# A full-attention stage rewritten per pair of 64-wide heads, with row-tiled scores and column-tiled weighted values

## The reference

```
def _L1_attn_ref(x, Wq, Wk, Wv, Wo, bo):
    S, D, H, DH, SCALE = 256, 128, 16, 64, 64 ** -0.5
    q = (x @ Wq).reshape(b, s, H, DH)      # Wq, Wk, Wv: 128 x 1024
    k = (x @ Wk).reshape(b, s, H, DH)
    v = (x @ Wv).reshape(b, s, H, DH)
    scores = jnp.einsum('bqhd,bkhd->bhqk', q, k) * SCALE
    attn = jax.nn.softmax(scores, axis=-1)
    out = jnp.einsum('bhqk,bkhd->bqhd', attn, v).reshape(b, s, H * DH)
    return out @ Wo + bo                   # Wo: 1024 x 128

x = x + _L1_attn_ref(_layernorm(x, axis=-1), ...)   # no scale or shift in the norm
```

## Time and profile before

| | before |
|---|---|
| median of 3 runs | 5669.12 us (5667.3 to 5673.87) |
| profiled execution, its own time | 5667.65 us |
| its span, first to last instruction | 5665.8 us |
| granted TensorE clock over the span | 0.962 |
| PE busy | 4785.3 us (84%) |
| DVE busy | 4254.1 us (75%) |
| ACT busy | 3789.1 us (67%) |

### The profile page before, as it was taken

One profiled execution on the slowest core, in us unless ns is written; L12 is line 12 of the kernel. 1 busy time (PEld: TensorE's weight loads), 2 busy tenths in 40 slices (PEclk: granted clock), 3 DMA queues, 4 the chain that ended last, 5 costly groups with the idle time before them and its releaser, 6 DMA issues.

```text
span 5665.8 us, 133229 instructions
## 1 busy us (share of the span) xinstructions
PE 4785.3 (84%) x47928; PEld 3219.6 (57%) x48122; DVE 4254.1 (75%) x6024; ACT 3789.1 (67%) x7196; POOL 2480.3 (44%) x1142
## 2 busy tenths in 40 slices
PE   3349999999958888888888888888888888888886
PEld 1124478888835555555555555555555555555554
DVE  6761155566678888888888888888888888888886
ACT  3323255555547777777777777777777777777775
POOL 0100000000046565665656656565665656566564
PEclk7669999999979999999999999999999999999998
DMA  2000000000010000000000000000000000000001
GB/s 59 0 0 0 0 20 0 0 0 0 0 39 0 0 0 0 19 0 0 0 0 19 0 0 0 4 15 0 0 0 19 0 0 0 0 19 0 0 0 34
DMA packets 43314, 34.86 MB, mean 6 GB/s; under 512 B 3771, under 2 KB 39062, under 8 KB 42262
## 3 DMA queue, kind: packets, MB, share of 16 engines
q1 hardware_dynamic: 43286, 34.52, 2.0%
HBM read 30.32 MB, written 4.19 MB: 6 GB/s over the span
## 4 chain that ended last, share of the span: by engine, by line
PE 44%; DVE 22%; issue 16%; ACT 9%; DVEq 2%; ACTq 0%; POOL 0%; DMA 0%; SPq 0%; POOLq 0%
DVE arena L927 6%; PE bank L1356 5%; PE bank L1446 5%; PE bank L802 4%; PE bank L766 4%; DVE arena L948 4%; PE bank L534 4%; DVE arena L955 4%; PE bank L1404 4%; PE bank L1382 4%; ACT arena L1174 3%; PE bank L753 2%; PE bank L757 2%; PE bank L787 2%; DVE arena L965 2%
## 5 line engine op out<-in xcount | busy, mean ns | idle before, releaser
L1298 POOL TENSOR_TENSOR arena<-arena,rope_d 128x512 f32<-128x512 f32 x780 | 1296.2, 1693 | 1000.3 <-DVE arena L936 1000.3
L1304 POOL TENSOR_TENSOR arena<-arena 128x2048 f32<-128x2048 f32 x195 | 898.8, 4609 | 424.5 <-DVE arena L948 407.4
L1404 PE MATMUL bank<-m_vo,arena 128*32 128x512 f32 x6144 | 743.8, 603 | 171.0 <-ACT arena L1174 168.5
L948 DVE TENSOR_TENSOR arena<-arena,rope_d 128x1024 f32<-128x1024 f32 x390 | 728.9, 1889 | 13.4
L1356 PE MATMUL bank<-wqk_split,x_split 128*128 (+1 forms) x2352 | 670.9, 421 | 15.9 <-ACT arena L1122 11.0
L1122 ACT ACTIVATE arena<-bank 128x512 f32<-128x512 f32 x784 | 453.3, 598 | 324.8 <-PE bank L1356 303.3
L1280 POOL TENSOR_TENSOR rope_d<-rope,qk_scale 128x128 f32 (+1 forms) x14 | 6.4, 457 | 1228.7 <-DVE x_all L1022 1228.7
L1366 PE MATMUL bank<-ident,arena 128*128 128x128 f32 x3104 | 435.8, 284 | 120.6 <-ACT arena L1145 65.0
L1404 PEld LDWEIGHTS bank<-m_vo,arena 128*32 128x32 f32 x6144 | 160.3, 109 | 621.8 <-ACT arena L1174 484.6
L1356 PEld LDWEIGHTS bank<-wqk_split,x_split 128*128 128x128 f32 x2352 | 430.4, 190 | 134.6 <-issue 19.7
L927 DVE TENSOR_REDUCE arena<-arena 128x16 f32<-128x1024 f32 x390 | 455.4, 1209 | 7.7 <-ACT arena L1129 7.7
(11 more groups left out here) (228 smaller groups left out, 9327.2 us busy)
## 6 DMA issues: line engine op xcount, KB each, us to landing
wqk_stage<-in_wqk SPq DMA_DIRECT2D x8, 1024.0 KB, 6.9
out_x<-x_all SPq DMA_DIRECT2D x8, 512.0 KB, 5.4
wvt<-in_wvt SPq DMA_DIRECT2D x7, 512.0 KB, 4.0
wo<-in_wo SPq DMA_DIRECT2D x7, 512.0 KB, 5.2
w<-in_w SPq DMA_DIRECT2D x7, 341.0 KB
arena<-in_wbh SPq DMA_DIRECT2D x1, 2048.0 KB, 9.9
arena<-out_x SPq DMA_DIRECT2D x4, 512.0 KB, 5.8
w<-in_w SPq DMA_DIRECT2D x7, 128.0 KB
```

The lines of the kernel that those rows point to most:

```text
L948: nc.vector.tensor_tensor(d_rot[j][:, m * H:(m + 1) * H, :], d_raw[j][:, m * H:(m + 1) * H, :], tab, ALU.mult)\
L1298: last = nc.gpsimd.tensor_tensor(d_t2[:, m * H:(m + 1) * H, a:a + half], d_raw[j][:, m * H:(m + 1) * H, z:z + half], rope_d[:, bass.ds(par ...
L1304: nc.gpsimd.tensor_tensor(d_rot[j], d_rot[j], d_t2, ALU.add).then_inc(s_rope, 1)
L1404: last = nc.tensor.matmul(bank[6 + w % 2][q * WIN:(q + 1) * WIN, :], d_xv[:, w * WIN:(w + 1) * WIN], m_vo[:, 4 * q:4 * q + 4, :].rearrange ...
```

## The change

Stage C now forms q, k and v. The unit of work is a pair of heads over all 256 queries, so a sequence has 8 turns (`TURNS = PAIRS`) and the stage 128.

- The weights are transposed once (24 transposes) into `c_wq`, `c_wk`, `c_wv`; the per-head products and `c_a`, `c_z`, `c_u` are gone from this stage.
- q and k of a pair (2 x 64 rows) are made by two full matmuls, with all channels as contraction (`queries_keys`). Scores are four matmuls with a contraction of 64: head 0 uses rows 0 to 63 of the array, head 1 rows 64 to 127 (row tiling), and each head has a bank of its own.
- Weighted values are four matmuls with 64 output columns: head 0 to partitions 0 to 63, head 1 to 64 to 127 of one bank (column tiling, `tile_position`). They come out as (head channel x query), ScalarE copies them to `c_ot`, and once per sequence `output` multiplies them by Wo, a new step of 16 matmuls and 2 bias matmuls.
- The two reads of transposed probabilities are shared: head 0 by ScalarE, head 1 by VectorE.
- Probabilities have two slots instead of four.
- The first two and the last two sequences stand outside the loop, so that no work is done for sequences beyond the last.
- SP no longer waits for the products before it loads stage D's first layer.

The core of the diff (removed functions stand above; semaphore bookkeeping is left out):

```diff
-        TURNS = TPS * PAIRS
-        HALF = TURNS // 2
-        RING = 4
+        TURNS = PAIRS
+        UNITS = 14
+        V_TURNS = {2: 0, 3: 1, 4: 2, 5: 3}
+        OUT_TURN, XT_TURN = 1, 6
...
             def maximum(g, r):
+                for hd in range(2):
+                    dve.wait_ge(c_s, 2 * g + hd + 1)
+                    last = nc.vector.tensor_reduce(out=c_nm[:, r, hd, :], in_=score_bank(r, hd)[:, :].rearrange("p (j k) -> p j k", j=TPS),
+                                                   op=ALU.max, axis=AXX, negate=True)
+                last.then_inc(c_max, 1)
...
+            def sequence_turns(n, s, left):
+                for t in range(TURNS):
+                    g = n * TURNS + t
+                    read_probabilities(g, t % 2)
+                    if left > 0 or t + 1 < TURNS:
+                        probabilities(g + 1, (t + 1) % 2)
+                    if left > 0 or t + 2 < TURNS:
+                        maximum(g + 2, t % 2)
+                    if t == OUT_TURN and has_second(n, left, t):
+                        residual(n - 1, unit(n, left, t, True))
+                    if t in V_TURNS and left > 0:
+                        dve.wait_ge(c_unit, unit(n, left, t, True) + 1)
+                        read_v(c_v[1 - s], V_TURNS[t], bank[7]).then_inc(c_free, 1)
...
         def phase_c_scalar(act):
...
+                    read_probabilities(g, t % 2)
+                    if t > 0:
+                        read_outputs(g - 1, c_ot[s], t - 1)
...
+                    if left > 0:
+                        act.wait_ge(c_unit, unit(n, left, t, False) + 1)
+                        read_qk(c_qk[1 - s], t, bank[7]).then_inc(c_free, 1)
+                    if left > 0 or t + 2 < TURNS:
+                        exponentials(g + 2, t % 2)
+                    if t == XT_TURN and left > 1:
...
         def phase_c_tensor(pe):
...
+            def queries_keys(into, par, a):
+                for m, w in enumerate((c_wq, c_wk)):
+                    last = nc.tensor.matmul(into[:, m * T:(m + 1) * T], w[:, a * P:(a + 1) * P], c_xt[:, par, :], start=True, stop=True)
+            def scores(g, r, par, a):
+                wait_past(pe, c_exp, g - 1)
+                for j in range(TPS):
+                    for hd in range(2):
+                        rows = slice(hd * DH, (hd + 1) * DH)
+                        last = nc.tensor.matmul(score_bank(r, hd)[:, j * T:(j + 1) * T], c_qk[par][rows, a, 0, j * P:(j + 1) * P],
+                                                c_qk[par][rows, a, 1, :], start=True, stop=True)
+            def attend(g, r, par, a):
+                pe.wait_ge(c_pt0, g + 1)
+                pe.wait_ge(c_pt1, g + 1)
+                wait_past(pe, c_o_ready, g)
+                for k in range(TPS):
+                    for hd in range(2):
+                        h = 2 * a + hd
+                        last = nc.tensor.matmul(bank[6][hd * DH:(hd + 1) * DH, 0:T], c_v[par][:, k, h * DH:(h + 1) * DH],
+                                                c_pt[:, r, hd, k, :], start=(k == 0), stop=(k == TPS - 1), skip_group_check=True,
+                                                tile_position=(0, hd * DH))
+            def output(n, par):
+                pe.wait_ge(c_o_ready, TURNS * (n + 1))
+                for j in range(TPS):
+                    for a in range(PAIRS):
+                        nc.tensor.matmul(bank[7][:, j * C:(j + 1) * C], c_ot[par][:, a, j * P:(j + 1) * P], wo_c[:, a, :],
+                                         start=(a == 0), stop=False)
+                    last = nc.tensor.matmul(bank[7][:, j * C:(j + 1) * C], ones_row[:, :], bo[:, :], start=False, stop=True)
...
+            for m in range(2):
+                transpose_tokens(m, bank[6 + m]).then_inc(c_xtp, 1)
...
             sp.wait_ge(const_ready, CONSTS)
-            sp.wait_ge(loaded_c, LOADS_C * 16)
-            sp.wait_ge(c_m, 4)
             load_qk(sp, 0)
```

More of the change, by code:

```diff
@@ L593, in head_products, with unit, has_second, score_bank @@
                 last.then_inc(ready, 1)
[L595 to L601, removed]
+        def unit(n, left, t, second):
+            index = 0
+            for u in range(t + 1):
+                if left > 0 and (u < t or second):
+                    index += 1
+                if u < t and has_second(n, left, u):
+                    index += 1
+            if isinstance(n, int) and n == 0:
+                return index
+            return n * UNITS - 1 - (1 if left == 0 else 0) + index
+        def has_second(n, left, t):
+            if t == OUT_TURN:
+                return not (isinstance(n, int) and n == 0)
+            return left > 0 and t in V_TURNS or left > 1 and t == XT_TURN
+        def score_bank(g, hd):
+            return bank[2 * (g % 2) + hd]
+        def prob_bank(hd):
+            return bank[4 + hd]
+        def wait_past(eng, s, count):
+            if not (isinstance(count, int) and count < 1):
+                eng.wait_ge(s, count)
+        def sequences_c(eng, turns):
+            for s in range(2):
+                turns(s, s, 2)
+            with eng.Fori(1, SEQS // 2 - 1) as two:
+                for s in range(2):
+                    turns(two * 2 + s, s, 2)
+            for s in range(2):
+                turns(SEQS - 2 + s, s, 1 - s)
         def phase_c_vector(dve):
[L605 to L608, removed]
             link = Chain(dve, c_chain, 5, 0)
@@ L658, in phase_c_vector @@
             probabilities(0, 0)
[L659 to L674, removed]
@@ L734, in transpose_tokens @@
+            def transpose_tokens(m, into):
                 pe.wait_ge(c_xn_ready, m + 1)
                 for t in range(TPS):
[L736 to L746, removed]
[L747 to L759 removed]
@@ new lines, in transpose_tokens, with values @@
+                    last = nc.tensor.transpose(into[:, t * P:(t + 1) * P], c_xn[:, t, :], ident[:, :])
+                return last
+            def queries_keys(into, par, a):
+                for m, w in enumerate((c_wq, c_wk)):
+                    last = nc.tensor.matmul(into[:, m * T:(m + 1) * T], w[:, a * P:(a + 1) * P], c_xt[:, par, :], start=True, stop=True)
+                return last
+            def values(into, par, v):
+                k, half = v // 2, v % 2
+                return nc.tensor.matmul(into[:, :], c_xt[:, par, k * P:(k + 1) * P], c_wv[:, half * 512:(half + 1) * 512],
+                                        start=True, stop=True)
@@ L823, in build @@
+            sequences_c(pe, sequence_turns)
+            pe.wait_ge(c_free, unit(SEQS - 1, 0, OUT_TURN, True) + 1)
+            output(SEQS - 1, 1).then_inc(c_unit, 1)
         ld = Local()
```

260 lines of the change are left out of this document (140 added, 120 removed).

## The result

| | before | after |
|---|---|---|
| median | 5670.28 us (4 runs) | 5546.07 us (4 runs, 5542.91 to 5548.17) |
| profiled execution: span, clock | 5665.8 us, 0.962 | 5546.4 us, 0.957 |
| stage C, first transpose or product to the last residual | 837.4 us | 716.5 us |
| stage D and the rest behind it | 4107 us | 4107 us |

The ratio is 0.9781 (95% interval 0.9768 to 0.9795): faster, by 124 us in the medians. The forecast was 5548 us. The span shrank by 119.4 us and stage C by 120.9; the 1.5 us between them is stages A and B, which ended that much later in this execution. Stage D did not move, so SP's earlier loads cost and gave nothing that can be seen.

A forecast was written before the change was run, and what follows sets the result against it. Stage C was taken as bound by the columns PE streams. 14 sequences of 43.2 us, first 38, last 36 and end 6 gave 685 against 803.9; with 2 from the prologue, 121 saved: 5548 us, range 5528 to 5595.

The forecast's parts named there:

- The bound and the unit of count: Stage C: bound by columns PE streams, counted as passes at 0.11 us per 128 columns.
- The slower rival: Stage C scores and weighted values: neither 64-wide form overlaps, 198 us above forecast, 5746 us; chance 0.06.
- The tilings stream abreast: Stage C scores and weighted values: tiles stream side by side, 0.87 us each per turn instead of 1.74.
- two rivals on serial streaming: Stage C tilings: only row tiles serial, 5636 us, chance 0.06; or both forms serial, 5746 us, chance 0.06.
- the one on the order of passes: Stage C tiled matmuls: passes keep strict order, about 45 us more, 5593 us; chance 0.08.
- The change of tiling, 0.17: PE in stage C: each switch between whole and tiled array costs 0.17 us, four a turn, 0.69.
- The ring: Stage C, ACT and DVE: exponentials, scaling, next maximum, next exponentials take 4.86 us, falling behind PE in turns 6, 7, 0.
- Waits: Stage C, PE: weighted values wait behind late exponentials in turns 7, 0 and 1, 1.5 us a sequence.
- The sum: Stage C and prologue: 685 us against 803.9 saves 119, prologue saves 2, 121 in all; median 5548 us.
- the last sequence and the output behind it: End of stage C: last sequence bound by the engine loop, 36 us; then last copy, output and residual, 6.
- The first sequence: Start of stage C: no output of a predecessor and no wait before it, 38 us.
- The prologue: Before the stage C loop: first transpose at about 752.6, 2 us saved from 33.4, with 5 either way.

The follow-up runs named there:

- row_serial: Changed kernel with both heads' scores on array rows 0 to 63, undoing row tiling; ratio to the kernel before 0.9942, stage C 806.4 us.
- col_whole: Changed kernel with each head's weighted values on all 128 output columns, undoing column tiling; ratio to the kernel before 0.9877, stage C 767.9 us.
- both_serial: Changed kernel with both heads' scores on rows 0 to 63 and weighted values on the first 64 output columns; 5746.71 us, ratio to the kernel before 1.0132.
- qk_first: Changed kernel with queries and keys before the scores on PE; ratio to the kernel before 0.9825, stage C 732.9 us.
- ring_long: Changed kernel with VectorE taking head 0's maximum once more each turn into an unread tile; ratio to the kernel before 0.986, stage C 754.3 us.
- after_again: Changed kernel itself, unedited, run again on another chip as reference; ratio to the kernel before 0.9788, stage C 716.9 us.
- bias_vector: Changed kernel with the bias added to x by VectorE instead of two bias matmuls; ratio to the kernel before 0.9745, stage C 692.4 us.
- no_changes: Changed kernel with scores and weighted values each as two whole-array matmuls, without tiling; ratio to the kernel before 0.9729, stage C 683.7 us.

## Why the prediction was right, point by point

**The bound and the unit of count: right.** Streamed passes at 0.11 us per 128 columns set the time before and after; row_serial, col_whole and both_serial each moved the stage by the passes that they added. The slower rival had been given 5746 us and took 5746.71.

**The tilings stream abreast: right.** 0.87 each was taken, with a change in and out; 1.07 and 1.01 from start to start fit that. The two rivals on serial streaming and the one on the order of passes (0.22 more, twice a turn) are excluded by the rows of after. So is the rule of the Trainium skill (TensorE: Matmul & The Clock Gate, Part 3) that a weight load overlaps only where the row group differs: by it the weighted values would take about 0.2 more than forecast, and they take 1.01.

**The change of tiling, 0.17: right.** A turn with values takes 5.07, its passes 0.88 + 3 x 0.87 + 0.86 = 4.35, so four changes cost 0.72, that is 0.18 each. By my reading of the start-to-start distances each is about 0.09 ahead of the new form's first load and 0.10 (0.05 for 64 columns) behind it. Turn 2 of qk_first, which waits for nothing, takes 0.19 less than in the changed kernel: one direct change from row tiles to column tiles costs one, not two.

**The ring: right in kind, too long by 0.2.** I had 4.86. In the rows of after, four scalings take 1.14 and not 1.24, and two maxima 1.29 and not 1.38 (when the scores are there, the second instruction of a kind starts before the first has ended); one walk through the ring is 1.96 + 1.35 + 1.29 = 4.6. The loop shows it whole: after PE's shorter turns 6, 7 and 0 the exponentials of three turns running start 4.63 to 4.65 apart, each set waiting for the maximum. The timeline of all engines of the changed kernel, at its first turns, and in the loop the exponentials beside PE's turns 7 and 0:

```profile
750.67 0.47 ACT L741 ACTIVATE arena<-bank,arena 128x256 f32<-128x256 f32 x1 [5.22 <-DVE arena L661]
...
752.63 0.18 DVE L667 RECIPROCAL arena<-arena 128x4 f32<-128x4 f32 x1 [0.80 <-ACT arena L741]
...
752.84 1.14 DVE L671 TENSOR_SCALAR arena<-arena 128x256 f32<-128x256 f32 x4
...
758.11 1.29 DVE L661 TENSOR_REDUCE arena<-bank 128x2 f32<-128x512 f32 x2
...
1002.30 0.47 ACT L741 ACTIVATE arena<-bank,arena 128x256 f32<-128x256 f32 x1 [0.54 <-DVE arena L661]
...
1006.93 0.47 ACT L741 ACTIVATE arena<-bank,arena 128x256 f32<-128x256 f32 x1 [0.61 <-DVE arena L661]
```

Waits took 0.7 a sequence where I had 1.5 and PE's own work 41.9 where I had 41.7, so the middle sequences took 42.58 where I had 43.2. The wait in turn 7 was also not the one named: it is queries and keys on ScalarE's token copy (1003.31 to 1004.56, 0.2 late), a wait I had listed nowhere. ring_long shows that the slack is real and small: 0.6 more on the ring costs 2.5 a sequence.

**The sum: right by two errors that cancel.** The 14 middle sequences took 595.4 us, 9 less than forecast. The end took 8 more: the last sequence and the output behind it were given 42 and took 49.8. That the forecast came within 2 us of the median is luck to this extent. About 4 of the 8 are the last sequence itself, which took 40.4 up to the start of its output where I had 36 and a copy, and which ran in part at the lower clock too. The other 4 are the output: after a stretch in which PE waits for the ring (idle 2.44 at the most) the granted clock falls, and the final output runs at the 1.2 GHz level, 8.4 us where I had 4.6. The windows of the changed kernel (columns as in the windows above), and its PE's timeline behind them:

```profile
1410.00:1424.00 14.00, 10.08 (x66) 6.66 (x68) 9.98 (x26) 8.19 (x31) 0.00 (x0) 0.88 0.00 0
1424.00:1439.30 15.30, 13.35 (x60) 10.42 (x60) 1.49 (x4) 1.28 (x4) 0.00 (x0) 0.55 0.00 1
```

```profile
1427.30 1.97 PE L842 MATMUL bank<-arena 128*64 128x256 f32 x8 [0.83 <-DVE arena L678]
1429.83 3.76 PE L851 MATMUL bank<-arena 128*128 128x128 f32 x16 [0.56 <-ACT arena L753]
```

Sixteen passes take 3.7 here and 1.98 in the loop. after_again had the same (clock 0.57), bias_vector did not (1.00), with much the same gaps on PE ahead of it, and the other kernels fall on both sides; what decides it no run here settles. The first sequence took 39.9 for 38, its first turn partly at the low clock too. The prologue took 31.4, as forecast.

## What to carry to other kernels

When a busy engine is the bound, count what it streams in its own unit, and price a new form from any stage of the same trace that already uses it: here column tiles from stage D and a change of tiling from one bias matmul were enough to bring a turn with values within 0.03 us (5.04 for 5.07). Then look at what the shortened engine now runs beside: a ring over two engines that were 60% busy had 0.4 us left in the turns with values and none in turns 6, 7 and 0, and the cuts that shortened TensorE's already short turns (no_changes, qk_first) lost most or all of their worth to waits on those two. A small odd-shaped matmul in a stream of whole ones costs its two changes as well, so work of that kind is cheaper on an engine that is waiting anyway. And where engines run ahead of each other by a slot or two, a ring that is too long shows itself turns later than where it falls behind, so read its own pace, from one exponential to the next, and not only the bound engine's turns.

## What the runs showed of the hardware

- Row tiles of 64 stream fully abreast in fp32 also when four passes of one half come before four of the other: 1.07 us either way.
- A direct change from row tiles to column tiles costs one change (about 0.18), like one to the whole array: turn 2 takes 4.94 us with three changes (qk_first) and 5.13 with four (after).
- On one chip the unchanged stage D took 4123 to 4126 us in all four kernels profiled there, against 4103 to 4113 in all the others, 0.4% more.
